# Second layer's experts: ten dense experts per token become two dense shared experts and 71 tiles of rows scattered by expert

## What is computed

```python
def _gate(xf, gate_w, gate_bias):
    scores = jax.nn.sigmoid(xf @ gate_w)
    sfc = scores + gate_bias[None]                     # T x 8
    group_scores = jax.lax.top_k(sfc.reshape(T, 4, 2), 2)[0].sum(axis=-1)
    _, group_idx = jax.lax.top_k(group_scores, 2)      # 2 of 4 groups
    tmp_scores = jnp.where(score_mask > 0, sfc, 0.0)
    _, topk_idx = jax.lax.top_k(tmp_scores, 2)         # 2 of 8 experts
    topk_w = jnp.take_along_axis(sfc, topk_idx, axis=-1)
    topk_w = topk_w / (topk_w.sum(axis=-1, keepdims=True) + 1e-20)
    return (topk_idx, topk_w * 2.5)
g = jax.nn.silu(jnp.einsum('th,ehi->tei', xf, w_gate))      # 8 experts, hidden 128
u = jnp.einsum('th,ehi->tei', xf, w_up)
experts_y = jnp.einsum('tei,eih->teh', g * u, w_down)
y = sum of the two chosen experts' rows, weighted
shared = jax.nn.silu(x @ sw_gate) * (x @ sw_up) @ sw_down   # hidden 256
x = x + jnp.tanh(g_ffn[1]) * _L1_ffn_ref(_layernorm(x, axis=-1), ...)
```

## Time and profile before

| | |
|---|---|
| median of 3 runs | 3332.64 us (3330.05 to 3339.01) |
| the profiled execution's own time | 3338.82 us |
| its span, first to last instruction | 3337.1 us |
| PE busy over the span | 3069.5 us (92%), 21570 matmuls |
| DVE / ACT / POOL busy | 1762.7 (53%) / 1171.2 (35%) / 354.2 us (11%) |
| mean granted TensorE clock | 0.952 of full speed |
| DMA | 145.98 MB, 44 GB/s over the span |

### The profile page before, as it was taken

One profiled execution on the slowest core, in us unless ns is written; L12 is line 12 of the kernel. 1 busy time (PEld: TensorE's weight loads), 2 busy tenths in 40 slices (PEclk: granted clock), 3 DMA queues, 4 the chain that ended last, 5 costly groups with the idle time before them and its releaser, 6 DMA issues. The chain is left out here.

```text
span 3337.1 us, 58274 instructions
## 1 busy us (share of the span) xinstructions
PE 3069.5 (92%) x21570; PEld 2467.3 (74%) x21571; DVE 1762.7 (53%) x4396; ACT 1171.2 (35%) x2177; POOL 354.2 (11%) x647
## 2 busy tenths in 40 slices
PE   7969999999997998997999979999899989965998
PEld 6846666666665887886888866666578877755998
DVE  4537777777761114774656556777622227751111
ACT  1315555555552213441212113555423323322222
POOL 1101111111110000000000000101000001123111
PEclk9979999999997999997999988999999999957999
DMA  3010000000003441001000000000011100064554
GB/s 112 0 33 2 1 0 0 0 0 0 0 1 103 153 148 36 19 16 48 0 0 0 0 27 1 1 0 0 25 60 64 62 18 1 0 189 141 183 173 134
DMA packets 93093, 145.98 MB, mean 44 GB/s; under 512 B 12878, under 2 KB 74574, under 8 KB 86864
## 3 DMA queue, kind: packets, MB, share of 16 engines
q1 hardware_dynamic: 89600, 136.39, 12.9%
q0 software_dynamic: 3408, 8.46, 0.7%
HBM read 131.18 MB, written 14.56 MB: 44 GB/s over the span
## 5 line engine op out<-in xcount | busy, mean ns | idle before, releaser
L507 DVE TENSOR_REDUCE m0hnm<-banks 128x4 f32<-128x1024 f32 x256 | 312.9, 1222 | 172.9 <-PE banks L435 172.7
L534 ACT ACTIVATE m0hpT<-banks 128x1024 f32<-128x1024 f32 x256 | 262.7, 1026 | 355.4 <-PE banks L448 355.4
L435 PE MATMUL banks<-m0hk,m0hq 32*128 32x256 f32 x2048 | 292.7, 403 | 12.1 <-DVE m0hnm L507 11.7
L448 PE MATMUL banks<-m0hq,m0hk 32*128 32x256 f32 x2048 | 291.8, 402 | 1.1 <-ACT m0hpT L534 1.1
L532 ACT ACTIVATE a2hpT<-banks,a2hlow 128x512 f32<-128x512 f32 x256 | 161.9, 684 | 181.3 <-PE banks L448 181.3
L435 PEld LDWEIGHTS banks<-m0hk,m0hq 32*128 32x128 f32 x2048 | 176.0, 185 | 64.1 <-DVE m0hnm L507 33.3
L507 DVE TENSOR_REDUCE a2hnm<-banks 128x4 f32<-128x1024 f32 x128 | 156.7, 1224 | 95.5 <-PE banks L435 95.2
L448 PEld LDWEIGHTS banks<-m0hq,m0hk 32*128 32x128 f32 x2048 | 177.8, 185 | 2.1 <-issue 1.7
L1622 ACT ACTIVATE E1sg<-banks 128x256 f32<-128x256 f32 x160 | 61.3, 383 | 326.8 <-PE banks L1639 326.8
L1639 PE MATMUL banks<-e1xnT,E1wg 128*128 128x256 f32 x640 | 166.5, 383 | 0.0
L1639 PE MATMUL banks<-e1xnT,E1wu 128*128 128x256 f32 x640 | 165.1, 381 | 0.0
(11 more groups left out here) (400 smaller groups left out, 6249.5 us busy)
## 6 DMA issues: line engine op xcount, KB each, us to landing
E3w<-in_L_ffn_W_dram SPq DMA_DIRECT2D x47, 1024.0 KB, 5.2
E0w<-in_L_ffn_fw_dram SPq DMA_DIRECT2D x64, 512.0 KB, 4.6
E2w<-in_L_ffn_w_dram SPq DMA_DIRECT2D x16, 1024.0 KB, 7.3
slots_x<-E3zeros SPq DMA_DIRECT2D x1, 5070.0 KB, 25.4
E3xin<-slots_x SPq DMA_DIRECT2D x39, 130.0 KB, 2.0
ctx_in<-in_ctx_dram SPq DMA_DIRECT2D x16, 256.0 KB, 4.8
x_all<-in_x_dram SPq DMA_DIRECT2D x16, 256.0 KB, 5.0
A1ctx_in<-in_ctx_dram SPq DMA_DIRECT2D x16, 256.0 KB, 2.6
```

Source lines behind the costliest of these rows:

```text
L435: ins = pe.matmul(self.scores[:, j, tc], self.q[strip(half, j), u, e, c, chunk(tc)], self.k[strip(half, j), u, e, c], start=True, stop=True)
L448: ins = pe.matmul(self.turned[:, j, kc], self.k[strip(half, j), u2, e2, c2, chunk(kc)], self.q[strip(half, j), u2, e2, c2], start=True, st ...
L507: v.tensor_reduce(self.nm[:, e, :, at:at + 33:32].rearrange("p c g -> p g c"), self.scores, AX.X, ALU.max, negate=True).then_inc(self.nm_r ...
L534: ins = a.activation(dst, self.turned, ACT.Exp)
```

## The change

`layer1_experts` is rewritten, in two parts.

First part, pairs i = 0 to 7 unrolled: normalised rows go to `rows_x` (a ring of 4 pairs), are transposed into `env.n2T` (kept for all sequences) and give logits and choice as before. Only the shared expert is computed here: `up` and `down` for two sequences, two halves (e = 0, 1) each, one Silu, one `gated` and one `add_up` per sequence. `ranks` counts on PE which place each token has in each chosen expert's region: a product with the triangular matrix `below`, one with `ones` for the running count `run`, and three more for the blocks before. `places` turns that into two slot numbers and two weights for each token. POOL then sends each block of 128 rows twice to DRAM (`scatter`: 8 indirect DMAs per pair, 64 in all), into a region of `CAP` rows for each of the eight experts. POOL also computes the reciprocal roots of the layer norm (`roots`).

Between the parts: total counts per expert, a table of the expert (`owner`) and first row (`base`) of each of 71 tiles, and eight DMAs of padding rows behind each region's end (`tail`).

Second part: 71 tiles of 128 rows, unrolled. SP reads `base[t]` into a register and loads the tile (`xin`, a ring of 6). PE transposes the rows, multiplies them by the owner's gate and up weights (rows are the stationary side now, so one product gives 128 rows x 256), ACT takes Silu of the 128x128 gate half, DVE the product, PE transposes that and multiplies by the owner's down weights. ACT scales by the row's weight into `yo` (a ring of `YR` = 4), POOL scatters it to row 2 * token or 2 * token + 1 of a DRAM tensor `routed`. `aside` on DVE works out which of the two it is and with which weight, and waits until the scatter of tile t - 4 has landed.

`layer2_attention` loads both rows of each token (`routed`, 512 KB per sequence, from SP) and adds them to x ahead of `stats` (two operations of DVE on 128x512 and a short memset for each sequence). `stats(0)` now stands ahead of the wait for the weights. The weights of the changed stage are laid out on the host so that a partition's row is one run, in 10 loads, of which only 8 small ones are waited for at first. The constant `count` grows from 40 to 72 columns.

```diff
@@ -1481,196 +1481,477 @@
...
+    CAP = B * S + T
+    TILES = (2 * B * S + E * (T - 1)) // T
...
+    RP, XR, YR = 4, 6, 4
...
+            sp.wait_ge(tail_rdy, 1)
+            for e in range(E):
+                at = sp.value_load(tail[0:1, e:e + 1], min_val=0, max_val=E * CAP - T)
+                sp.dma_start(slots[bass.ds(at, T)], pad[:]).then_inc(fill_in, 16)
...
+            for t in range(TILES):
+                at = sp.value_load(base[0:1, t:t + 1], min_val=0, max_val=E * CAP)
+                if t >= XR:
+                    sp.wait_ge(side_rdy, t - XR + 1)
+                    sp.wait_ge(xT_mm, t - XR + 1)
+                sp.dma_start(xin[:, t % XR], slots[bass.ds(at, T)]).then_inc(x_in[t % XR], 16)
...
+            def roots(i):
+                for u in (0, 1):
+                    b = 2 * i + u
+                    g.wait_ge(mv_rdy, b + 1)
+                    g.tensor_tensor(rstd[:, u], mv[:, u, :, 1], env.eps5[:], ALU.add).then_inc(var_rdy, 1)
+                    g.wait_ge(var_rdy, b + 1)
+                    g.tensor_tensor(rstd[:, u], rstd[:, u], env.mhalf[:, 0:C], ALU.pow).then_inc(rstd_rdy, 1)
+
+            def scatter(i):
+                g.wait_ge(row_rdy, i + 1)
+                for j in range(R):
+                    n = R * i + j
+                    for k in range(2):
+                        g.indirect_dma_start(slots, bass.IndirectOffsetOnAxis(ap=slot[:, k, n:n + 1], axis=0),
...
+            for i in range(NI):
+                if i >= 1:
+                    scatter(i - 1)
+                if i + 2 < NI:
+                    roots(i + 2)
+            scatter(NI - 1)
+
+            for t in range(TILES):
+                g.wait_ge(yo_rdy, t + 1)
+                g.indirect_dma_start(routed, bass.IndirectOffsetOnAxis(ap=idx[:, t % YR:t % YR + 1], axis=0), yo[:, t % YR], None,
+                                     bounds_check=2 * B * S - 1, oob_is_err=False).then_inc(put[t % YR], 16)
...
+            def normalised(i):
+                if i >= RP:
+                    v.wait_ge(sent[i % RP], 16 * 2 * R * (i // RP))
+                for u in (0, 1):
+                    b = 2 * i + u
+                    v.wait_ge(rstd_rdy, b + 1)
+                    for c in range(C):
+                        last = v.tensor_scalar(rows_x[:, i % RP, C * u + c, 0:D], env.x[:, b, c], mv[:, u, c, 0:1], rstd[:, u, c:c + 1],
+                                               ALU.subtract, ALU.mult)
+                    last.then_inc(xn_rdy, 1)
...
+            def choice(i):
+                first_of(v, ch, sel[:], tmp[:], first[:], gt[:], eq[:], E, 2).then_inc(hot_rdy, 1)
+                v.wait_ge(hot_rdy, i + 1)
+                v.tensor_tensor(wt[:], sel[:], sfc[:], ALU.mult)
+                ch.link(v.tensor_reduce(add[:], sel[:].rearrange("p r e -> p e r"), AX.X, ALU.add))
+                if i >= 1:
+                    v.wait_ge(rank_mm, i)
+                v.tensor_tensor(run[:, 1 - i % 2], run[:, i % 2], add[:], ALU.add)
...
+            def places(i):
+                here = rows_x[:, i % RP]
+                v.wait_ge(rank_mm, i + 1)
+                ch.link(v.tensor_tensor(pos[:], rank_bank.rearrange("p (r e) -> p r e", e=E),
+                                        ecap[:].unsqueeze(1).broadcast_to([P, R, E]), ALU.add))
+                v.sem_inc(rank_used, 1)
+                ch.link(v.tensor_tensor(pos[:], pos[:], sel[:], ALU.mult))
+                v.tensor_reduce(both[:], pos[:], AX.X, ALU.add)
+                ch.link(v.tensor_reduce(here[:, :, D + 1], pos[:], AX.X, ALU.max))
+                v.tensor_copy(here[:, :, D], tok2[:, R * i:R * i + R])
+                v.tensor_copy(slot[:, 0, R * i:R * i + R], here[:, :, D + 1])
+                v.tensor_tensor(slot[:, 1, R * i:R * i + R], both[:], here[:, :, D + 1], ALU.subtract)
+                ch.link(v.tensor_tensor(mine[:], pos[:], wide(here[:, :, D + 1]), ALU.is_equal))
...
+            for i in range(NI):
+                groups(i)
+                gated(i, 0)
+                if i >= 1:
+                    places(i - 1)
+                gated(i, 1)
+                choice(i)
+                if i + 2 < NI:
+                    moments(i + 2)
+                for u in (0, 1):
+                    add_up(i, u)
+                if i + 2 < NI:
+                    normalised(i + 2)
+            places(NI - 1)
...
+            def turned(t):
+                v.wait_ge(xT_mm, t + 1)
+                if t >= 3:
+                    v.wait_ge(tgu_mm, t - 2)
+                v.tensor_copy(xT[:, t % 3], env.ps[:, t % 2, 0:C * T].rearrange("p (c t) -> p c t", c=C)).then_inc(xT_rdy, 1)
+
+            def aside(t):
+                x, j = xin[:, t % XR], t % YR
+                v.wait_ge(x_in[t % XR], 16 * (t // XR + 1))
+                if t >= YR:
+                    v.wait_ge(put[j], 16 * (t // YR))
+                ch.link(v.tensor_tensor(high[:, j:j + 1], x[:, D + 1:D + 2], own[:, t:t + 1], ALU.is_equal))
+                v.tensor_tensor(idx[:, j:j + 1], x[:, D:D + 1], high[:, j:j + 1], ALU.add)
+                v.tensor_scalar(wy[:, j:j + 1], high[:, j:j + 1], x[:, D + 3:D + 4], x[:, D + 2:D + 3], ALU.mult, ALU.add)\
+                    .then_inc(side_rdy, 1)
+
+            def product_of(t):
+                v.wait_ge(silu_rdy, t + 1)
+                if t >= 2:
+                    v.wait_ge(hTr_mm, t - 1)
+                v.tensor_tensor(h[:, t % 2], env.ps[:, 2 + t % 2, I:2 * I], silu[:, t % 2], ALU.mult).then_inc(th_rdy, 1)
...
+                aside(t)
+                product_of(t)
+                if t + 2 < TILES:
+                    turned(t + 2)
...
+            def weighted(t):
+                a.wait_ge(side_rdy, t + 1)
+                a.wait_ge(ty_mm, t + 1)
+                a.activation(yo[:, t % YR], env.ps[:, 6 + t % 2, 0:D], ACT.Identity, scale=wy[:, t % YR:t % YR + 1])\
+                    .then_inc(yo_rdy, 1)
...
-                for half, wt_ in ((0, wg), (1, wu)):
-                    for k in range(C):
-                        last = pe.matmul(bank(4 * (e % 2) + u)[:, half], wt_[:, e, k], fr.xnT[:, u, k],
-                                         start=(k == 0), stop=(k == C - 1))
-                last.then_inc(gu_mm, 1)
...
+            def up(i, u):
+                b = 2 * i + u
+                pe.wait_ge(xnT_rdy, b + 1)
+                for e in range(2):
+                    for half in range(2):
+                        for k in range(C):
+                            last = pe.matmul(gu_banks(u)[:, e, S * half:S * half + S], sgu[:, k, half, e], xnT[:, b, k],
+                                             start=(k == 0), stop=(k == C - 1))
+                last.then_inc(gu_mm, 1)
+
+            def down(i, u):
+                b = 2 * i + u
+                pe.wait_ge(h_rdy, b + 1)
+                if i >= 1:
+                    pe.wait_ge(y_used, b - 1)
+                for tc in range(C):
+                    for e in range(2):
+                        last = pe.matmul(y_bank(u)[:, tc], hT[:, u, e, chunk(tc)], sd[:, e], start=(e == 0), stop=(e == 1))
+                last.then_inc(y_mm, 1)
+
+            def ranks(i):
+
+                pe.wait_ge(hot_rdy, i + 1)
+                pe.wait_ge(sc_rdy, 2 * min(i + 1, NI - 1) + 1)
+                if i >= 1:
+                    pe.wait_ge(rank_used, i)
+                flat = sel[:].rearrange("p r e -> p (r e)")
+                pe.matmul(rank_bank, below[:], flat, start=True, stop=False, skip_group_check=True)
+                pe.matmul(rank_bank.rearrange("p (r e) -> p r e", e=E), ones[:],
+                          run[:, i % 2].unsqueeze(1).broadcast_to([P, R, E]), start=False, stop=False, skip_group_check=True)
+                for j in range(R - 1):
+                    last = pe.matmul(rank_bank[:, (j + 1) * E:].rearrange("p (r e) -> p r e", e=E), ones[:],
...
+                down(i, 0)
+                down(i, 1)
+                if i + 1 < NI:
+                    turn(i + 1)
+                    logits(i + 1)
+                ranks(i)
...
+            def owner_of(t):
+                return bass.ds(pe.value_load(owner[0:1, t:t + 1], min_val=0, max_val=E - 1), 1)
...
+            def tile_up(t):
+                e = owner_of(t)
+                pe.wait_ge(xT_rdy, t + 1)
+                if t >= 2:
+                    pe.wait_ge(th_rdy, t - 1)
+                for k in range(C):
+                    last = pe.matmul(env.ps[:, 2 + t % 2, 0:2 * I], xT[:, t % 3, k], wgu[:, e, k].rearrange("p e i -> p (e i)"),
+                                     start=(k == 0), stop=(k == C - 1))
+                last.then_inc(tgu_mm, 1)
+
+            def hidden_turn(t):
+                pe.wait_ge(th_rdy, t + 1)
+                if t >= 2:
+                    pe.wait_ge(hTr_rdy, t - 1)
+                pe.transpose(env.ps[:, 4 + t % 2, 0:T], h[:, t % 2], env.ident[:]).then_inc(hTr_mm, 1)
+
+            def tile_down(t):
+                e = owner_of(t)
```

(44 more changed lines are left out.)

345 lines of the change are left out of this document (222 added, 123 removed).

## The result

The changed kernel takes 3235.69 us (median of four runs, 3233.88 to 3239.63), the one before 3331.81 us (3330.05 to 3339.01): ratio 0.9709, 95% interval 0.9692 to 0.9726. The forecast was 3246 us, 10 us too high. The profiled execution took 3239.63 us against 3338.8 us, 99.2 us less, and the trace says where these come from. First the stage itself, in four stretches: opening until the places of pair 0 begin, from there to the end of the places of pair 5, the last two pairs with their scatters until the first tile, tiles and drain. Columns are the stretch, its length, the busy time (and instructions) of each engine, the granted clock of TensorE, the DMA share and GB/s.

A forecast was written before the change was run, and what follows sets the result against it. PE alone was taken to bound the old stage. Profiled 3338.8 - 109.3 (stage) + 22.5 (stage after) = 3252.0; the median lies 6.2 lower: 3246 us. Own range 3205 to 3290; 8 in 10: 3195 to 3325.

The forecast's parts named there:

- First part: Pairs of the changed stage: opening 36, pairs 1 to 5 97, last two 23, scatters 13.8, first tile 2.9; 172.7 us.
- the loop: First part: POOL's scatters, roots, DVE's norm, groups and places wait on each other in turn; 19.4 us a pair.
- My next limits: First part, work per pair if the loop did not bind: DVE 15.2 us, PE near 15 us.
- The 215 us: Length of the changed stage if PE stayed the bound in both parts, which the prediction did not expect.
- Second part: 71 tiles at 2.3 us, 163.3, plus filling 0.8, drain 8 and half clock at both parts' starts 3; 175.1 us.
- The ring: Second part: four output rows, each waiting for the scatter four tiles before; 2.15 us a tile, 3.2 with slow landings.
- The drain: End of the second part: two products, weighting, scatter, landing and barrier; 8 us.
- The stage after: Adding routed rows on DVE ahead of the maximum PE waits for: 1.5 us a sequence, 22.5 us; bounds 0 and 27.
- Faster loop: Rival, second part: sequencer's loads overlap better, POOL's 1.8 us is the tile's period; 35 us less, 3211; chance 0.12.
- Slow landings: Rival, second part: scatters land in 5.7 us as in the last stage, period 3.2; 64 us more, 3310; chance 0.13.
- Held scatters: Rival, first part: scatters wait for half of DVE's work, loop about 27 us; 50 us more, 3296; chance 0.09.
- Half clock: Rival, both parts: gaps keep PE at the lower clock, pair 29 us, tile 3.3; 3394, slower than before; chance 0.09.

The follow-up runs named there:

- the roots ahead: Changed kernel with POOL issuing the roots of pair i+2 ahead of the scatters of pair i-1: 3245.1 us, ratio 0.9743; run again 3253.72 us, ratio 0.9763.
- the combinations: Changed kernel with one register load a tile, ring of eight, POOL's additions, split padding, extra drain: 3174.79 us; the same with the roots ahead: 3183.33 us.
- the repeated changed kernel: The changed kernel profiled once more, unaltered, on another chip than the four variants tried first: 3238.51 us, ratio 0.9713 against the kernel before.

## Why the prediction came out

**First part.** Forecast 36 + 97 + 23 + 13.8 + 2.9; measured 36.1, 92.2, 22.8, 13.5 and 3.2 us (each counted to the end of the places named), 167.7 instead of 172.7. The only term off is the loop, 18.4 us for 19.4: POOL's launch behind `places` takes 0.3 us (1578.74 to 1579.03), not 0.9, the eight scatters 9.9, not 10.2. The loop was the cause: the roots ahead take DVE's wait away and the pair goes to 16.6 us. My next limits, 15.2 and 15 us, left out that TensorE, once it has gaps, does part of its ups at the lower clock level: the one pair at a granted clock of 1.00 took 15.1. The 215 us that I gave for a stage bound by TensorE alone is a slip, since eight pairs of 14.4 us and 116 for the tiles are 231; nothing hangs on it.

**Second part.** Forecast 0.8 + 163.3 + 8 + 3 for 71 tiles of 2.3 us; measured 179.8 us instead of 175.1. The pace is right, and so is its cause, though no run shows by itself the 0.2 us that I gave to semaphore waits: a register load on PE's sequencer has a median of 0.30 us by itself and about 0.65 us to the next wait, two a tile; taking one away brings 0.6 us once the ring gives way too. The ring was put at 2.15 and measures 2.05, the array 1.63 and 1.65 to 1.69. Filling took 2.0 us, with the first tile's up products at half clock (2.07 us, where later ones take 1.12). The 3 us for the half clock had no other use; the stretch of the tiles has a granted clock of 0.96. The drain failed: from tile 70's first product to the next stage's start it is 16.0 us, where the forecast has 2.3 + 8, and of these POOL's own drain, from the landing of the last output scatter (1863.9) to 1870.7, is 6.8, for which the forecast had nothing but a barrier.

**The stage after.** This term was mis-sized by half: 10.8 us, not 22.5. The mechanism is the one named, additions ahead of a maximum without slack, and with them off DVE all 1.06 us of it go. But they cost 1.06 us a sequence, not 1.5. From the end of the first maximum to the start of the second DVE takes 3.04 us (2109.34 to 2112.38) instead of 1.88 (2214.42 to 2216.30): the additions take 1.45, but the update behind them 0.72 instead of 0.91 and the rest 0.1 less. TensorE had 0.1 us to give. And eleven periods pay it, not 15: from the first update to the twelfth, 11 x 1.06 is 11.7 us. What comes ahead of the first update is 0.45 us shorter than before the change (91.15 us for 91.60), and what comes after the twelfth 0.4 (76.5 for 76.9), which leaves the 10.8. Between the bounds of 0 and 27 us the value was taken near the upper; the row of a plain addition, 0.69, was the better guide for each, and the opening and the last periods should have been left out.

**The rivals.** Faster loop: the sequencer does not get ahead; mean periods under 1.8 us came only when a load was taken away and the ring made longer. Slow landings: 2.4 us at the median, 3.4 at most; the 1 MB loads to which I laid the 5.7 of the last stage are absent here, but no run tests that reason. Held scatters: 0.96 us each as in the earlier trace rows, with DVE busy for 69.6 of 94.4 us beside them; none of 64 took more than 1.23 us. So the rival is out. By the rule of the Trainium skill ("SBUF — State Buffer", section "SBUF: two separate sides") POOL can't write a DMA's descriptors while DVE runs an instruction in a two-port mode, and the DMA appears blocked. No view shows DVE's mode, so the rule itself stays untested. The loop of the changed kernel keeps `normalised` clear of the scatters; with the roots ahead it runs beside them (from 1580.22 for 1.50 us; the scatters at 1580.28 and 1581.62 took 1.04 and 0.96), and these aren't held either. Half clock: 0.96 in the tiles, 0.87 in the pairs; it comes, but beside POOL's loop, where it costs nothing. With the roots ahead it costs 1.5 us a pair.

**What would have shown it.** Pairs 19 us apart with `normalised` waiting for POOL, tiles 2.3 us apart with TensorE idle for "issue": both there. `aside` not waiting for the scatter: wrong, and harmless. The maximum 1.5 us later and the stage after 22 us longer: 1.16 and 10.8. "Unrolled code that stalls the sequencers, which no row bounds": no stall in the changed kernel's profile, but instructions 1 to 10 us late in variants of it, of which the cause is open.

## What to carry to other kernels

When two limits lie within a tenth of each other, an engine's waits name the one that happens to come last and not the one that pays: size each limit by taking the other away (here 0.05 us for the ring alone, 0.26 for a register load alone, 0.62 for both). In a pipeline over engines, look for the loop that a queue's order closes before summing up the engines, and for what the next stage pays for work moved to it: there a sum by place (how many sequences really run without slack) is worth more than one more decimal in the operation. And before a fix is counted, run it: the order of the roots was right about the loop and the kernel took 8.5 us more all the same with everything else equal (the combinations, on one chip), 9 and 18 us more in the two runs without the rest, on chips with a late first tile.

## What was not expected of the hardware

- POOL's drain at the end of a stage waits for more than the landing of its scatters: it ended 8.8 us after the start of the last of 135 (6.8 us after its landing), and 6.8 to 6.9 us after that of the last of 71, about 0.03 us for each; all engines stand at the barrier for it.
- Sixteen scatters of 128 rows in a row (20 us), on two of the chips: instructions of ACT and DVE with all they wait for in place came up to 10.6 us late, SP's took up to 0.7 us instead of 0.02. Eight with a pause of 6 us did so less: on those two chips single exponentials of ACT in the pairs came 1 to 3 us late; in the first profile and on the chip of the repeated changed kernel none did by more than 0.7, and there the last sixteen in a row held up nothing either. So sixteen alone are not enough, and what is held up is open. The Trainium skill ("Runtime: NRT & Kernel Launch", section "Instruction fetch mechanics") says that a sequencer fetches its code ahead over a DMA queue of its own and that this is mostly hidden in straight code; the transfers of the two instruction queues that the profile lists all lie outside the three long standstills, and no run here shows one that waits.
- A register load of TensorE's sequencer, which hides behind queued matmuls in the last stage, sets the pace here, with nine array products and transposes a tile: 0.30 us by itself, about 0.65 to the next wait, and 0.57 us a tile less (2.26 to 1.69) with one of two taken away.
